# Residual stack of four layers: W1 on ScalarE's queue, the coefficient chain on GpSimd, transposes of the quantized quarters one product later

## The chip, the cores and the metric

The kernel runs on one core of a Trainium2 chip. The metric is the device time of one execution in microseconds (us); lower is better. Engines are named as in the profile: PE is TensorE, DVE is VectorE, ACT is ScalarE, POOL is GpSimd, SP is SyncE, which only issues transfers. Each runs its own list of instructions in order and waits on semaphores for the others.

## The reference, cut to what matters

`x` is (64, 64, 1024) in fp32: batch, head or row, position. Four layers each add to it:

```python
x = x + L0(x)   # y = irfft(rfft(u*mask) * rfft(K)), K = 2*einsum('hn,hnl->hl', Cs, exp(dtA*l)).real ; + u*D, masked
x = x + L1(x)   # x @ W1.T + 2 * (top-2 gated experts, each of rank 16: h = x @ A_e.T, then B_e)
x = x + L2(x)   # x @ W2.T + 0.5 * (x @ lora_A[label]) @ lora_B_w.T
x = x + L3(x)   # x @ w_eff.T
# L0: dt = exp(log_dt); A = -exp(log_A_real) + 1j*A_imag; dtA = A*dt; Cs = C*(exp(dtA)-1)/A     (64 x 64 each)
# L3: lora = B3 @ A3 ; wg = W3 + lora ; q = codebook[searchsorted(thresholds, wg/scale)]*scale ; w_eff = q + lora
```

## The kernel before

The three dense layers are linear in x, so the kernel multiplies their matrices once and then makes one pass over x. Up to about 370 us it builds the matrix and the tables of the convolution; after that it runs 32 alike tiles of two rows each.

**Preparation, in PE's order** (the list `order`, from which every engine takes its own part):

- `b3t` transposes B3; with A3 it gives the low-rank product of layer 3 in four quarters, `delta` (q = 0 to 3). It leaves in `dq`.
- `w2t` transposes a row block of W2 into `A2`; `qt(kt)` multiplies one column block of (1 + W2) by `E1` = (1 + W1 | 2·B_lang), 24 products: 16 of 512 columns, 8 of 128. The unit matrix is added by POOL, one 128x128 diagonal block at a time (`e1_ready`, `a2_ready`).
- `codesT`, `codes` sort out the code book; `nat4` transposes the four 64-column tables of layer 0; `at`, `wrt` transpose the expert matrices.
- `a3(q, n)` transposes the finished quarter q of the quantized matrix in four pieces, and `m(q, mt)`, ten products for each quarter, multiplies it into the final matrix `Mh`, `Ml`.
- Pieces leave PSUM through two alternating banks (`stage`): a piece waits until ACT has taken the one two before it.

**DVE** first works on the code book (`places_ready`), splits B3 and A3 (`b3_lo`), exponentiates the scale, then has a chain of about 70 instructions of 64x64 for layer 0 (lines 1376 to 1424, `exps`, `nat`, `nat4`), then the masks. Then come the four quarters of W3: two additions and a product over `vq`; for each code book step kept (here nine) two `TENSOR_SCALAR` (L1459) and two `TENSOR_TENSOR` (L1464) of 128x1024, here called the rises; a tail of four instructions (L1504, L1505). After the last quarter DVE builds the tables of layer 0 (`theta`, `rem`, `expo`) from `tabs`, together with sines and exponentials on ACT.

**POOL** adds the diagonals, and for quarters 0 to 2 runs `finish_quarter(q)`, three instructions that scale the quarter and add `dq`; `m_lo` is its subtraction behind each `m`. **ACT** takes pieces out of PSUM; `init_quarter(q)` fills the quarter's tile with the first code, and DVE's rises wait for it:

```python
                        if kt in (3, 4, 6):
                            init_quarter((3, 4, 6).index(kt) + 1)
```

**SP** issues all loads in the order of its code; W1's eight blocks come behind ten smaller loads.

Of the kernel before, what the change touches and what calls it, by code (L numbers as in the profile page):

```python
# [39 lines left out]
def resid_stack_kernel(nc, x, lengths, languages, labels, codebook, log_dt, C_ri, log_A_real, A_imag, D_skip,  # L40
# [96 lines left out]
    B3n = place("B3n", [P, NC, 2, R3], F32, at=region_q + 4 * (5 * QCOLS + 2 * 1024))  # L137
# [23 lines left out]
    nat = place("nat", [H, 16, N], F32, at=region_carry + 4 * 2 * EW)  # L161
    logs = place("logs", [H, 1 + N], F32)
# [3 lines left out]
    ex = place("ex", [P, 6, H + 1], F32)  # L166
    ex_bits = place("ex_bits", [P, H + 1], I32)
# [55 lines left out]
    with ExitStack() as ctx:  # L223
# [6 lines left out]
        ld_b3, ld_rank, ld_w1, ld_blang, ld_la = sem("ld_b3"), sem("ld_rank"), sem("ld_w1"), sem("ld_blang"), sem("ld_la")  # L230
# [6 lines left out]
        nat_rem, nat_sin, nat4_ready = sem("nat_rem"), sem("nat_sin"), sem("nat4_ready")  # L237
# [20 lines left out]
        order = [("b3t", 0), ("b3t", 1), ("codesT",)] + deltas(0) + [("w2t", 0, 0), ("w2t", 0, 1)]  # L258
        between = {0: [("codes",)], 1: [("nat4",), ("at", 0), ("at", 1), ("wrt",)], 2: deltas(1), 5: deltas(2), NC - 1: deltas(3)}
# [4 lines left out]
        order += [("a3", 0, n) for n in range(4)] + [("lap", mt) for mt in range(MT)]  # L264
# [5 lines left out]
        jobs = [j for j in order if j[0] not in ("qt", "m")]  # L270
# [61 lines left out]
        with nc.Block() as block:  # L332

            @block.sync
            def _(sp):
# [35 lines left out]

                load_w2(0)
                load_w2(1)
                for it in range(NC):
                    sp.dma_start(E1[:, it, L:EW].rearrange("p (e r) -> p e r", e=E),
                                 B_lang[:, it * P:(it + 1) * P, :].rearrange("e o r -> o e r")).then_inc(ld_blang, 16)
                for t in range(QT_TILES):
                    load_w3(0, t)
                sp.dma_start(len_i[:, :], bass.AP(lengths.tensor, 0, [[0, P], [1, B]])).then_inc(ld_ids, 16)
                for hh in range(HB):  # L380
                    rows = slice(hh * B, (hh + 1) * B)
                    sp.dma_start(ids_i[rows, 0:1], languages.rearrange("(b a) -> b a", a=1)).then_inc(ld_ids, 16)
                    sp.dma_start(ids_i[rows, 1:2], labels.rearrange("(b a) -> b a", a=1)).then_inc(ld_ids, 16)
# [55 lines left out]
            def _(pool):  # L439
# [74 lines left out]
                for it in range(NC):  # L514
# [11 lines left out]
                    if it == NC - 3:  # L526
                        finish_quarter(0)
# [60 lines left out]
            def _(pe):  # L588
# [1034 lines left out]
```

## Time and profile before

| | |
|---|---|
| median of 3 runs | 1046.71 us (1045.72 to 1048.4) |
| the profiled execution | 1049.61 us, of it 1047.8 us from first to last instruction (the span) |
| mean granted clock of TensorE | 0.992 |
| busy: PE, DVE, ACT, POOL | 1004.1, 850.6, 428.5, 292.0 us |

The span starts with the first instruction. All moments below are microseconds from there. A busy share is an average over the stages; what counts for a change is which engine another one waits for in its own stage.

### The profile page before, as it was taken

How to read it: one execution, taken by the hardware profiler on the slowest of the kernel's cores; microseconds unless marked ns; L12 is line 12 of the kernel's file. 1: busy time of each engine (PE TensorE's matmuls, PEld its weight loads, DVE VectorE, ACT ScalarE, POOL GpSimd, SP SyncE). 2: the span in 40 equal slices, each digit the busy share in tenths (PEclk: the TensorE clock that was granted, in tenths of full speed). 3: DMA queues.
4: the chain of work that ended last, by engine and by line, in shares of the span. 5: the costliest groups of instructions: out<-in, count | busy, mean ns of one | idle time of the engine just before them, and what ended most of it. 6: DMA issues, size and time to landing. Idle time of an engine off the chain costs nothing.

```text
span 1047.8 us, 16630 instructions
## 1 busy us (share of the span) xinstructions
PE 1004.1 (96%) x4855; PEld 800.8 (76%) x4855; DVE 850.6 (81%) x1678; ACT 428.5 (41%) x847; POOL 292.0 (28%) x319
## 2 busy tenths in 40 slices
PE   2999999999899999999999999999999999999997
PEld 1555556978688878888888888888888888888885
DVE  5888888979896488878888888888888888888862
ACT  3212222222257454454445444544354535553531
POOL 2200304373435323222332233222322232223100
PEclk9999999999999999999999999999999999999999
DMA  8601000010201335454544455445544454445311
GB/s 257 164 21 61 20 6 35 1 41 1 40 1 21 64 59 104 80 89 75 104 84 84 77 103 87 79 81 97 94 76 84 88 100 74 88 81 103 59 39 41
DMA packets 316659, 74.97 MB, mean 72 GB/s; under 512 B 292490, under 2 KB 309194, under 8 KB 316626
## 3 DMA queue, kind: packets, MB, share of 16 engines
q1 hardware_dynamic: 316626, 74.56, 36.2%
q8 instruction: 16, 0.26, 0.1%
q14 instruction: 17, 0.14, 0.0%
HBM read 57.61 MB, written 16.91 MB: 71 GB/s over the span
## 4 chain that ended last, share of the span: by engine, by line
PE 75%; DVE 10%; issue 9%; ACT 2%; DMA 2%; DVEq 1%; SPq 0%; ACTq 0%
PE bank L647 33%; PE bank L637 10%; PE bank L774 6%; PE bank L823 5%; PE bank L668 4%; PE bank L617 4%; PE bank L606 4%; PE bank L628 3%; DVE quant L1464 3%; PE bank L674 2%; DVE step_t L1459 1%; DVE quant L1505 1%; DVE vq L1478 1%; PE bank L658 1%; DVE quant L1504 1%
## 5 line engine op out<-in xcount | busy, mean ns | idle before, releaser
L647 PE MATMUL bank<-Mh,strips_r 128*128 128x512 f32 x1024 | 289.9, 395 | 0.0
L647 PEld LDWEIGHTS bank<-Mh,strips_r 128*128 128x128 f32 x1024 | 190.7, 188 | 41.5
L475 POOL TENSOR_TENSOR Cl<-QC,Ch 128x256 fp32r<-128x256 f32 x32 | 36.9, 1152 | 454.5 <-ACT Ch L879 454.5
L647 PE MATMUL bank<-Ml,strips_r 128*128 128x512 f32 x512 | 160.6, 395 | 0.0
L897 ACT ACTIVATE SK<-ZZ 64x448 f32<-64x448 f32 x128 | 73.9, 577 | 211.1 <-DVE ZZ L1182 208.7
L1182 DVE SCALAR_TENSOR_TENSOR ZZ<-ZZ,coef 128x192 f32<-128x192 f32 (+1 forms) x256 | 120.3, 510 | 10.1 <-DVE ZZ L1173 0.3
L774 PE MATMUL bank<-E,A 128*128 128x512 f32 (+1 forms) x384 | 126.2, 489 | 0.0
L647 PEld LDWEIGHTS bank<-Ml,strips_r 128*128 128x128 f32 x512 | 96.2, 188 | 22.5
L774 PEld LDWEIGHTS bank<-E,A 128*128 128x128 f32 x384 | 63.9, 192 | 61.8 <-issue 61.8
L637 PE MATMUL bank<-Mh,strips_r 128*128 128x296 f32 x512 | 110.5, 299 | 0.2 <-DVE strips_r L1201 0.2
L1464 DVE TENSOR_TENSOR quant<-quant,step_t 128x1024 f32<-128x1024 f32 x72 | 92.4, 1323 | 0.0
L637 PEld LDWEIGHTS bank<-Mh,strips_r 128*128 128x128 f32 x512 | 85.1, 189 | 5.4 <-issue 5.2
L1173 DVE SCALAR_TENSOR_TENSOR ZZ<-ZZ,coef 128x384 f32<-128x384 f32 (+1 forms) x128 | 80.3, 627 | 7.0 <-issue 1.0
L1459 DVE TENSOR_SCALAR step_t<-vq,steps 128x1024 f32<-128x1024 f32 x72 | 66.9, 970 | 21.7 <-DVEq L1499 13.1
L637 PE MATMUL bank<-Ml,strips_r 128*128 128x296 f32 x256 | 76.9, 300 | 0.0
L888 ACT ACTIVATE ZZ<-bank 64x448 f32<-64x448 f32 x128 | 68.5, 535 | 2.6 <-PE bank L606 0.3
L823 PE MATMUL bank<-A3b,QT 128*128 128x256 f32 x288 | 65.4, 387 | 3.7 <-ACT A3b L966 3.2
L823 PE MATMUL bank<-A3a,QT 128*128 128x256 f32 x288 | 65.2, 386 | 0.0
L823 PEld LDWEIGHTS bank<-A3b,QT 128*128 128x128 f32 x288 | 55.3, 194 | 12.0 <-ACT A3b L966 3.6
L1153 DVE TENSOR_TENSOR strips_r<-strips,strips_r 128x512 fp32r<-128x512 f32 x64 | 59.0, 924 | 5.7 <-ACT strips_r L867 5.7
L823 PEld LDWEIGHTS bank<-A3a,QT 128*128 128x128 f32 x288 | 55.5, 195 | 7.6
L1239 DVE TENSOR_TENSOR hgTl<-bank,hgTh 128x128 fp32r<-128x128 f32 x32 | 9.3, 292 | 61.3 <-ACT hgTh L918 61.3
(279 smaller groups left out, 1733.8 us busy)
## 6 DMA issues: line engine op xcount, KB each, us to landing
X<-in_x SPq DMA_DIRECT2D x256, 64.0 KB, 2.6
XT<-in_x SPq DMA_DIRECT2D x256, 64.0 KB, 2.5
out_x<-O SPq DMA_DIRECT2D x64, 256.0 KB, 3.2
toep<-kpad SPq DMA_DIRECT2D x128, 64.0 KB, 2.1
E<-in_L_cond_W SPq DMA_DIRECT2D x8, 512.0 KB, 7.4
W2s<-in_L_cond_W SPq DMA_DIRECT2D x8, 512.0 KB, 4.4
vq<-in_L_cond_weight SPq DMA_DIRECT2D x8, 512.0 KB, 3.3
LA<-in_L_cond_lora_A SPq DMA_DIRECT2D x8, 80.0 KB, 3.4
```

The costliest lines, as they stand in the source:

```text
L606: last = pe.matmul(psZ[hh][:, 0:SB].rearrange("p (c b) -> p c b", b=B), (Bh, Bl)[w][:, hh, :], (xh, xl)[p][:, 0:NC - 1, hh * B:(hh + 1) * ...
L637: last = pe.matmul(psL[:, 0:LOWC], xs[:, c, :], ms[:, c, L:MW], start=(c == 0 and n == 0), stop=False, skip_group_check=True)
L647: pe.matmul(psO[nh][:, :], xs[:, c, :], ms[:, c, nh * BANK:(nh + 1) * BANK], start=(c == 0 and n == 0), stop=False)
L774: last = pe.matmul(bank[s + n][:, 0:b - a], A2[:, it, kt * P:(kt + 1) * P], E1[:, it, a:b], start=(it == 0), stop=(it == NC - 1))
L823: last = pe.matmul(m_bank(n)[0:rows, 0:QO], lhs, A3[q % 2][:, kt, :], start=(kt == 0), stop=(kt == NC - 1))
L888: act.activation(ZZ[hh * N:(hh + 1) * N, :, ri, :], psZ[hh][ri * N:(ri + 1) * N, 0:SB].rearrange("p (c b) -> p c b", b=B), ACT.Copy).then_ ...
L897: act.activation(SK[ri * N:(ri + 1) * N, hh, :].rearrange("p (c b) -> p c b", b=B), ZZ[hh * N:(hh + 1) * N, :, ri, :], ACT.Copy).then_inc( ...
L1153: dve.tensor_tensor(xl[:, :, cols], xq[:, :, cols], xh[:, :, cols].bitcast(F32), ALU.subtract).then_inc(xl_done, 1)
L1173: dve.scalar_tensor_tensor(ZZ[:, dst, :, :], ZZ[:, src, :, :], coef[:, bass.ds(i, 1), power, 0], ZZ[:, dst, :, :], ALU.mult, ALU.add).then ...
L1182: dve.scalar_tensor_tensor(ZZ[:, dst, to, :], ZZ[:, src, of, :], coef[:, bass.ds(i, 1), power, n], ZZ[:, dst, to, :], ALU.mult, ALU.add).t ...
L1459: dve.tensor_scalar(step_t[:, c, :], vf[:, c * CH:(c + 1) * CH], kept_tau[:, bass.ds(k, 1)], rise[:, bass.ds(k, 1)], ALU.is_gt, ALU.mult). ...
L1464: dve.tensor_tensor(qf[:, cols], qf[:, cols], step_t[:, c, :], ALU.add).then_inc(dve_step, 1)
```

## The change

1. ACT issues W1's eight loads as its first instructions, each with its own semaphore `ld_w1[it]`. B3 is loaded once instead of twice, with 2 KB runs, and its copy of the transposed rows is made on ACT. SP's other loads change their order: W2 and W3 come ahead of `B_lang`, and the four loads of layer 0 come behind `B_lang`, after waits on `b3_lo` and `a3_pad`.
2. `qt(0)` is cut: `qt0(0)` multiplies blocks 0 to 3 of W1 as they come, ahead of `codesT` and `delta`; `qt0(1)` multiplies blocks 4 to 7 behind them.
3. Layer 0's chain leaves DVE for POOL as 90 instructions in four pieces (`nat_angles` 33, `nat_step` 30, `nat_products` 9, `nat_columns` 18; POOL's are split where DVE's did a product and an addition in one). Each piece stands between two of POOL's `a2_diagonal`. One reciprocal stays on DVE, ahead of quarter 1, behind a wait on `nat_den`. ACT's three sines move from behind `w2t(1)` to behind its take of `qt(1)`; `nat4` moves behind `qt(4)`.
4. `a3(q + 1, n)` stands behind `m` 3, 5, 7, 8 instead of 2, 4, 6, 8. `deltas(3)` moves behind `lap`. `init_quarter` moves from kt 3, 4, 6 to 3, 5, 7; `finish_quarter(0)` goes behind `a2_diagonal(5)`, `finish_quarter(2)` from behind `m(0, 4)` to behind `m(0, 8)`; `sines(0)` and `exponentials()` one product later.

```diff
-        order = [("b3t", 0), ("b3t", 1), ("codesT",)] + deltas(0) + [("w2t", 0, 0), ("w2t", 0, 1)]
-        between = {0: [("codes",)], 1: [("nat4",), ("at", 0), ("at", 1), ("wrt",)], 2: deltas(1), 5: deltas(2), NC - 1: deltas(3)}
+        order = [("b3t", 0), ("b3t", 1), ("w2t", 0, 0), ("w2t", 0, 1), ("qt0", 0), ("codesT",)] + deltas(0) + [("qt0", 1), ("codes",)]
+        between = {1: [("at", 0), ("at", 1), ("wrt",)], 2: deltas(1), 4: [("nat4",)], 5: deltas(2)}
...
-                if q + 1 < QUARTERS and mt in (2, 4, 6, 8):
-                    order += [("a3", q + 1, mt // 2 - 1)]
+                if q + 1 < QUARTERS and mt in (3, 5, 7, 8):
+                    order += [("a3", q + 1, (3, 5, 7, 8).index(mt))]
...
+                def exp_to(dst, src, w):
...
+                    step(pool.tensor_scalar(t[5], t[4], 1.0 / math.factorial(7), None, ALU.mult))
+                    for n in range(6, 0, -1):
+                        step(pool.tensor_scalar(t[5], t[5], 1.0 / math.factorial(n), None, ALU.add))
+                        step(pool.tensor_tensor(t[5], t[5], t[4], ALU.mult))
...
+                e1_diagonal(0)
+                e1_diagonal(1)
+
+                pool.wait_ge(e1_ready, 2)
+                pool.wait_ge(ld_a3, 32)
+                pool.tensor_tensor(A3lo[R3:, :], A3raw[R3:, :], A3raw[R3:, :], ALU.subtract).then_inc(a3_pad, 1)
+                pool.wait_ge(a3_pad, 1)
+                a2_diagonal(0)
+                for it in range(2, NC):
+                    e1_diagonal(it)
...
+                a2_diagonal(1)
+                pool.wait_ge(e1_ready, NC + 1)
+                pool.wait_ge(a2_ready, 2)
+                nat_angles()
+                a2_diagonal(2)
...
+                nat_step()
+                a2_diagonal(3)
+                pool.wait_ge(a2_ready, 4)
+                nat_products()
+                pool.wait_ge(nat_den, 1)
+                a2_diagonal(4)
+                pool.wait_ge(a2_ready, 5)
+                nat_columns()
+                a2_diagonal(5)
+                finish_quarter(0)
...
-                        if j == ("m", 0, 4):
+                        if j == ("m", 0, 8):
                             finish_quarter(2)
+                            pool.wait_ge(quant_done, 3)
...
+                for it in range(NC):
+                    act.dma_start(E1[:, it, 0:L], W1[it * P:(it + 1) * P, :]).then_inc(ld_w1[it], 16)
...
-                        if kt in (3, 4, 6):
-                            init_quarter((3, 4, 6).index(kt) + 1)
+                        if kt == 1:
+                            nat_sine()
+                        elif kt in (3, 5, 7):
+                            init_quarter(kt // 2)
...
+                    if q == 1:
+                        dve.wait_ge(nat_den, 1)
+                        dve.reciprocal(nat[:, 7, :], nat[:, 15, :]).then_inc(nat_inv, 1)
```

**PE at its start, before.** `ident` is the unit matrix used for transposes, `E_84` is `E1`, `A_85` is `A2`; ahead of these rows stand `b3t`, `codesT` and the first two `delta` pieces.

```order
L728 MATMUL bank<-A3hh,B3s 128x512 [waits stage_free]
L728 MATMUL bank<-A3lo,B3s 128x512
L733 MATMUL bank<-ident,W2s 128x128 [waits stage_free,ld_w2a]
L733 MATMUL bank<-ident,W2s 128x128 x3
L733 MATMUL bank<-ident,W2s 128x128 [waits stage_free]
L733 MATMUL bank<-ident,W2s 128x128 x3
L733 MATMUL bank<-ident,W2s 128x128 [waits stage_free,ld_w2b]
L733 MATMUL bank<-ident,W2s 128x128 x3
L733 MATMUL bank<-ident,W2s 128x128 [waits stage_free]
L733 MATMUL bank<-ident,W2s 128x128 x3
L774 MATMUL bank<-E_84,A_85 128x512 [waits stage_free,a2_ready,e1_ready]
L774 MATMUL bank<-E_84,A_85 128x512 x15
```

The same place with the change:

```order
L852 MATMUL bank<-ident,W2s 128x128 [waits stage_free]
L852 MATMUL bank<-ident,W2s 128x128 x3
L887 MATMUL bank<-E_84,A_85 128x512 [waits e1_ready,stage_free,a2_ready]
L887 MATMUL bank<-E_84,A_85 128x512
L887 MATMUL bank<-E_84,A_85 128x512 [waits e1_ready]
L887 MATMUL bank<-E_84,A_85 128x512
L887 MATMUL bank<-E_84,A_85 128x512 [waits e1_ready]
L887 MATMUL bank<-E_84,A_85 128x512
L887 MATMUL bank<-E_84,A_85 128x512 [waits e1_ready]
L887 MATMUL bank<-E_84,A_85 128x512
L858 MATMUL bank<-ident,cbw 64x128 [waits stage_free,places_ready]
L858 MATMUL bank<-ident,tau 64x128
```

Half of the first block's 512-column products now stands ahead of `codesT`; the eight `delta` products follow, then the other half, then `codes`.

**POOL at the diagonals of A2, before**: nothing stands between the diagonals of blocks 2 to 5 (the row with x4) and the finish of quarter 0.

```order
L517 TENSOR_TENSOR A_85<-A_85,ident 128x128 [waits stage_free]
L525 TENSOR_SCALAR Bw_64<-BwIn 128x8x32 [waits ld_rank]
L525 TENSOR_SCALAR Bw_64<-BwIn 128x8x32 x2
L517 TENSOR_TENSOR A_85<-A_85,ident 128x128 [waits stage_free] x4
L502 TENSOR_TENSOR quant_70<-quant_70,scale_82 128x1024 [waits v_used]
```

With the change, the end of `nat_step`, the diagonal of block 3, and the start of `nat_products`:

```order
L561 TENSOR_TENSOR nat<-nat 64x64 [waits pool_step]
L562 TENSOR_SCALAR nat<-nat 64x64 [waits pool_step]
L563 TENSOR_TENSOR nat<-nat 64x64 [waits pool_step]
L564 TENSOR_SCALAR nat<-nat 64x64 [waits pool_step]
L565 TENSOR_TENSOR nat<-nat 64x64 [waits pool_step]
L611 TENSOR_TENSOR A_85<-A_85,ident 128x128 [waits stage_free,pool_step]
L568 TENSOR_TENSOR nat<-c_in,nat 64x64 [waits a2_ready]
L569 TENSOR_TENSOR nat<-c_in,nat 64x64 [waits pool_step]
```

Block 3's diagonal, for which `qt(3)` waits, now stands behind 67 other instructions since the diagonal of block 1: 33 of `nat_angles`, block 2's diagonal, three of `Bw`, 30 of `nat_step`.

## Rows read from the trace of the kernel before

**Rows 1.** Page, part 1: busy time of each engine, share of the span, instructions.

```profile
PE 1004.1 (96%) x4855; PEld 800.8 (76%) x4855; DVE 850.6 (81%) x1678; ACT 428.5 (41%) x847; POOL 292.0 (28%) x319
```

**Rows 2.** Chain of work, 286 to 290 us: start, us, what.

```profile
286.26 2.71 DVE quant L1511
289.01 1.12 PE bank L790 x4
```

**Rows 3.** Timeline of PE: start, us, instruction, count, idle before and releaser.

```profile
21.16 0.79 PE L728 MATMUL bank<-A3hh,B3s 128*128 128x512 f32 x1 [1.65 <-DVE A3lo L1368]
28.19 15.68 PE L774 MATMUL bank<-E,A 128*128 128x512 f32 x48
45.88 15.68 PE L774 MATMUL bank<-E,A 128*128 128x512 f32 x48
...
66.33 13.90 PE L774 MATMUL bank<-E,A 128*128 128x512 f32 x30
...
87.21 15.68 PE L774 MATMUL bank<-E,A 128*128 128x512 f32 x48
...
236.47 10.63 PE L823 MATMUL bank<-A3b,QT 128*128 128x256 f32 x48 [3.15 <-ACT A3b L966]
...
289.01 1.12 PE L790 MATMUL bank<-ident,quant 128*128 128x128 f32 x4 [5.63 <-DVE quant L1511]
289.92 8.77 PE L823 MATMUL bank<-A3a,QT 128*128 128x256 f32 x32
...
298.96 7.07 PE L823 MATMUL bank<-A3a,QT 128*128 128x256 f32 x32
```

**Rows 4.** Timeline of DVE up to the rises of quarter 1, same columns.

```profile
26.62 0.19 DVE L1309 TENSOR_SCALAR ex<-logs 64x65 f32<-64x65 f32 x1
45.08 0.18 DVE L1429 CAST len_f<-len_i 128x64 f32<-128x64 int32 x1
48.48 2.49 DVE L1478 TENSOR_TENSOR vq<-vq,dq 128x1024 f32<-128x1024 f32 x2 [1.03 <-issue]
55.18 1.53 DVE L1459 TENSOR_SCALAR step_t<-vq,steps 128x1024 f32<-128x1024 f32 x2 [1.89 <-DVEq L1499]
97.04 1.22 DVE L1505 TENSOR_TENSOR quant<-quant,vq 128x1024 f32<-128x1024 f32 x1
107.58 2.30 DVE L1459 TENSOR_SCALAR step_t<-vq,steps 128x1024 f32<-128x1024 f32 x1 [2.18 <-DVEq L1499]
```

**Rows 5.** Busy time by stretch: the nine rises of quarters 0 to 3.

```profile
55.18:93.39 38.21, 36.09 (x134) 20.23 (x133) 34.02 (x37) 8.44 (x18) 1.62 (x2) 0.96 0.04 15
107.58:153.18 45.60, 44.41 (x143) 22.76 (x142) 41.67 (x36) 8.43 (x15) 10.55 (x5) 1.00 0.00 1
235.35:278.38 43.03, 41.91 (x202) 36.53 (x203) 39.10 (x37) 10.88 (x31) 18.12 (x17) 1.00 0.14 22
```

**Rows 6.** Timeline of POOL: one instruction alone, and the same kinds beside DVE.

```profile
21.27 3.40 POOL L513 TENSOR_TENSOR E<-E,ident 128x128 f32<-128x128 f32 x8 [10.68 <-DMA E<-in_L_cond_W]
66.40 1.17 POOL L517 TENSOR_TENSOR A<-A,ident 128x128 f32<-128x128 f32 x1 [20.04 <-ACT A L966]
175.82 1.92 POOL L543 TENSOR_TENSOR A3a<-A3a,ident 128x128 f32<-128x128 f32 x2 [8.71 <-ACT A3a L966]
332.02 0.61 POOL L452 TENSOR_TENSOR QB<-X1T,rem 128x256 f32<-128x256 f32 x1 [2.07 <-ACT coef L991]
```

**Rows 7.** Timeline of DVE beside POOL at 175 and at 220 us.

```profile
175.75 1.67 DVE L1459 TENSOR_SCALAR step_t<-vq,steps 128x1024 f32<-128x1024 f32 x2
220.02 2.80 DVE L1505 TENSOR_TENSOR quant<-quant,vq 128x1024 f32<-128x1024 f32 x1
226.13 5.24 DVE L1478 TENSOR_TENSOR vq<-vq,dq 128x1024 f32<-128x1024 f32 x1 [2.18 <-DMA vq<-in_L_cond_weight]
```

**Rows 8.** Timeline of ACT: the fill of quarter 1.

```profile
104.06 1.92 ACT L1009 ACTIVATE quant<-cb 128x2048 f32<-128x2048 f32 x1
```

**Rows 9.** Timeline of DVE: the second half of the tables.

```profile
320.11 1.56 DVE L1533 SCALAR_TENSOR_TENSOR rem<-theta 128x1344 f32<-128x1344 f32 x1 [3.13 <-ACT turns L975]
```

More of the change, by code:

```diff
@@ L159, in resid_stack_kernel @@
     Vt = place("Vt", [P, H, SPAN], F32, at=region_q - 4 * NC * QO)
[L161 to L162 removed]
+    logs = place("logs", [H, 1 + N], F32, at=region_q + 4 * (6 * QCOLS + 2 * 1024))
     exps = place("exps", [H, 1 + N], F32)
@@ L263, in resid_stack_kernel @@
             order += [("qt", kt)] + between.get(kt, [])
-        order += [("a3", 0, n) for n in range(4)] + [("lap", mt) for mt in range(MT)]
+        order += [("a3", 0, n) for n in range(4)] + [("lap", mt) for mt in range(MT)] + deltas(3)
         for q in range(QUARTERS):
@@ L758, in wrt, with qt0 @@
                     several(("wrt",), NC, lambda ps, c: pe.transpose(ps[:, c * E:(c + 1) * E], Wr_nat[:, c * P:(c + 1) * P], ident[0:E, 0:E]))
+                def qt0(part):
+                    if part == 0:
+                        pe.wait_ge(a2_ready, 1)
+                        pe.wait_ge(stage_free, jobno[("w2t", 0, 1)] + 1)
+                    for it in range(part * NC // 2, (part + 1) * NC // 2):
+                        pe.wait_ge(e1_ready, it + 1)
+                        for n in range(2):
+                            pe.matmul(bank[2 + n][:, :], A2[:, it, 0:P], E1[:, it, n * BANK:(n + 1) * BANK], start=(it == 0), stop=(it == NC - 1))
                 def qt(kt):
-                    if kt == 0:
-                        pe.wait_ge(e1_ready, NC)
                     pe.wait_ge(a2_ready, kt + 1)
@@ L824, in m @@
                     last.then_inc(m_full, 1)
-                do = dict(b3t=b3t, delta=delta, w2t=w2t, codesT=codes_t, codes=codes, nat4=nat4_t, at=at, wrt=wrt, qt=qt, lap=lap,
+                do = dict(b3t=b3t, delta=delta, w2t=w2t, codesT=codes_t, codes=codes, nat4=nat4_t, at=at, wrt=wrt, qt0=qt0, qt=qt, lap=lap,
                           a3=a3, m=m)
@@ L998, in _ @@
                 lo_n, hi_n = slice(0, N), slice(N, 2 * N)
+                for it in range(NC):
+                    act.dma_start(E1[:, it, 0:L], W1[it * P:(it + 1) * P, :]).then_inc(ld_w1[it], 16)
                 def nat_sine():
@@ L1013, in _ @@
                     if name == "b3t":
-                        take(j, B3raw[:, which[0] * BANK:(which[0] + 1) * BANK], stage(j)[0:2 * R3, :], scale=0.5)
+                        blocks = slice(4 * which[0], 4 * which[0] + 4)
+                        act.wait_ge(stage_full, jobno[j] + 1)
+                        for rows in (slice(0, R3), slice(R3, 2 * R3)):
+                            last = act.activation(B3raw[rows, :].rearrange("r (p t) -> r t p", t=NC)[:, blocks, :],
+                                                  stage(j)[0:R3, :].rearrange("r (t p) -> r t p", t=4), ACT.Copy, scale=0.5)
+                        last.then_inc(stage_free, 1)
                         if which[0] == 1:
@@ L1425, in _ @@
-                last.then_inc(nat4_ready, 1)
                 dve.wait_ge(ld_ids, 80)
```

218 lines of the change are left out of this document (126 added, 92 removed).

## The prediction

> **What bounds the kernel now.** I read the page first: PE is busy 96% of the span, DVE 81% [rows 1]. So the 32 tiles behind 370 us, which the change does not touch, are PE's, and only the 370 us of preparation can move. For these I read the chain of waits and then the timelines of PE, DVE, POOL and ACT side by side. The chain shows that preparation ends on DVE: its last addition for quarter 3 starts at 286.26, and PE's transposes of that quarter start at 289.01 [rows 2], after 5.63 us without work [rows 3]. PE has another stop of 3.15 us at 236.47 [rows 3]: ACT holds the last piece of `a3` back while POOL finishes quarter 2. Behind the 5.63 us the next two products take 8.77 us instead of 7.07, and the transposes 1.12 [rows 3]: 2.2 us more that the stop costs. Up to 289 PE and DVE are thus two strings of nearly the same length, PE's about 11 us shorter. A gain must come to both.
>
> DVE's string hangs on PE's in one place. The rises of quarter 1 start at 107.58 [rows 4], and the fill of their tile, which ACT does behind `qt(3)`, runs from 104.06 for 1.92 us [rows 8]: 1.6 us from its end to the rises.
>
> **Part 1: the opening.** Before, PE starts its first `delta` at 21.16, when DVE has split A3, and `qt(0)` at 28.19 [rows 3]. After, 16 of its 24 products are split in two, and the first half, about 7 us of the 15.68, stands in the idle time ahead of the `delta` pieces. The loads of W1 now run beside the scale's, for which DVE starts; I allow 1 us for that. PE: `delta` 22.2 to 26, second half to 33, `codes`, `w2t(1)`, the rest of `qt(0)` and `w2t(2)` to about 40; `qt(1)` starts there instead of at 45.88 [rows 3], about 6 us earlier. That `codes` is now free of `qt(0)`'s end, and that the chain of 26.62 to 45.08 has left DVE (18.5 us) [rows 4], brings DVE to quarter 0 at about 35.8 instead of 48.48: 12.7 us earlier.
>
> One rule speaks against moving W1: the Trainium skill, "DMA: Bandwidth & Descriptors", section "Rules for kernel authors", says that spreading transfers over several queues gives no bandwidth, only issue time. By it W1 cannot come early without making the scale late; if that took 3 us instead of 1, the sum below would be 2 us higher.
>
> **Part 2: the chain on POOL.** It starts with the diagonal of block 1, at about 35.5, so it lies beside DVE's quarter 0. What does one of its 64-column instructions take there? No row shows one. Alone, eight of 128 columns take 3.40 us, 0.43 each, and one of 256 takes 0.61 [rows 6]; for 64 I take 0.38 with its semaphore. Beside rises it is otherwise: the 128-column addition that met a DVE addition at 66.40 took 1.17, and two in a row at 175.82 took 1.92 [rows 6], while the DVE pair beside them took 1.67 instead of 1.53 [rows 7, 4]. Each time POOL's ends some 0.3 us after DVE's instruction does. So beside rises I count one POOL instruction for one of DVE's, and DVE loses little, 0.05 to 0.1 us each.
>
> Quarter 0 lasts from 48.48 to 98.26 [rows 4], 49.8 us, with 43 long DVE instructions (3, 36, 4), and about 7 us of gaps (1.89 ahead of the rises and 1.03 before the quarter [rows 4], 38.21 less 34.02 within the rises [rows 5]), in which 13 fit. So POOL does about 56 in 52.5 us. From this:
>
> - `nat_rem`, its 33rd: 30 us, at 66. ACT, in order, stands at its sines since `qt(1)` ended at 55.5; PE stops at `wrt`, two stage banks on. The sines, the take of `at`, then `wrt` and `w2t(3)` are some 4 of the 4.8 us that lie between the two blocks before (45.88 + 15.68 to 66.33 [rows 3]); with 2 us for a slow restart, as at 289, `qt(2)` starts at about 72, not 66.33. With 20.9 us from there to `qt(3)` (87.21 less 66.33) [rows 3] PE would be ready at 93.
> - Block 3's diagonal is the 68th: 12 are left when DVE's quarter ends at 88.3. DVE then waits for `nat_den`, and POOL goes at 0.4: 35.8 + 58.5 = 94.3.
> - So `qt(3)` starts at about 94.5, against 87.21: **+7.3**. DVE has `nat_den` at 98, and could start rises at 106, but ACT's fill comes behind `qt(3)`: rises at 107.58 + 7.3 = 114.9. DVE's 12.7 us are gone, and 7.3 more.
>
> The bounds of this step: with no wait at all, block 3's diagonal is early and `qt(3)` starts at 81 (-6); with a POOL instruction 15% dearer and a late opening, at 101 (+14). I take the middle, since both rows beside rises agree with one for one.
>
> **Part 3: behind `qt(3)`.** `nat_columns` lies in DVE's wait and costs nothing. `finish_quarter(0)` again meets the first rises (45.60 against 38.21 us for nine [rows 5]): 7.4 us, as before. `finish_quarter(2)` leaves the seam of quarters 2 and 3, where it made 1.22 into 2.80 and 5.24 [rows 4, 7], 5.6 us, and lands in the rises of quarter 3, 7.4 us: +1.8. Of the 4.8 us that subtractions cost those rises (43.03 against 38.21 [rows 5]) I take off 0.8. DVE is done at 289.0 + 7.3 + 1.0 = 297.3. PE, without the 3.15, arrives at the transposes at about 291.5 with one product more behind it: it waits again, but has 3.45 us less to do afterwards. **+7.3 + 1.0 - 3.45 = +4.85.** The tables follow DVE's end, +8.3, less the 3.13 us in which DVE waited for the sines [rows 9]: +5.2, as much as PE's. I cost the rest at nothing: `deltas(3)` is the same work for PE at either place and DVE wants it only at quarter 3's start, some 25 us later; the sines and exponentials one product later stand where PE, too, is one product further. If quarter 3 came as early as the first rival has it, that cover would still be over 10 us.
>
> The profiled execution has a span of 1047.8 and a time of 1049.61, the runs a median of 1046.71. +4.8 gives a span of 1052.6, and against the median **1051.5**.
>
> **The rivals.**
>
> - **The chain hides (faster).** If POOL gets two instructions in beside one of DVE's, `nat_rem` is there at 51, no engine stops, and `qt(3)` starts at 81: -6 + 1.0 - 3.45 = -8.4, 1038.3. For it: POOL's instructions are short. Against it: both of a pair at 175.82 waited. It decides below 0.6 us each. Chance 0.18.
> - **The instructions are cheaper, the queueing holds.** At 0.30 us each the gaps take more of them: `qt(3)` at 89.5, shift +2.3, end -0.2: no change, 1046.5. [...] No row here shows 64 columns. Chance 0.28.
> - **The opening slips as well (slower still).** If W1 beside SP's loads holds the scale, W2's block 2 or layer 0's loads back by 5 us, all of part 2 starts later: +10, 1056.7. Chance 0.12.
> - My forecast: 0.42.
>
> 0.3% is 3.1 us, about what a measurement tells from no change. Faster: the first rival and a little, 0.2. Same: the second and the forecast's lower edge (its own range 1047.5 to 1056), 0.3. Slower: 0.5. The range takes in the first rival's value and the last's: 1037.5 to 1059.
>
> **What would show it.** In the profile after: `qt(1)` from about 40 and quarter 0 from about 36 (part 1); POOL's 64-column rows at about 1 us beside rises and 0.4 when DVE stands; PE idle before `wrt` by about 10 us, behind ACT's sines; DVE idle before its reciprocal by about 10 us, with POOL as releaser; rises of quarter 1 at about 115; PE idle before the first transpose of quarter 3 by 5 us. I am wrong if POOL's rows are at 0.4 to 0.6 beside rises: then PE doesn't stop at `wrt`, and the end is earlier by up to 13 us.

## The result, and the profile after

The changed kernel takes 1070.96 us (median of 4 runs, 1067.71 to 1075.32) where the kernel before takes 1046.86 beside it: a ratio of 1.0232, interval 1.0191 to 1.0273. It is slower by 24 us. The forecast was 1051.5, with 1059 as the end of its range. The profiled execution has a span of 1070.4 and a time of 1072.25.

The page's busy line of the changed kernel, which answers to [rows 1]:

```profile
PE 1010.1 (94%) x4855; PEld 805.8 (75%) x4855; DVE 835.7 (78%) x1613; ACT 431.4 (40%) x849; POOL 351.5 (33%) x409
```

PE's share fell from 96 to 94% in a longer span. Of the 22.6 us by which the span grew, 16.6 are idle time of PE, and 6.0 are the same 4855 products taking longer (1010.1 against 1004.1 us busy, at a mean granted clock of 0.978 against 0.992). So the place to look is where PE stops, and how it starts again. PE's timeline of the changed kernel (start, time taken, engine, line, operation, count, and in brackets the idle time before it with what ended it), as [rows 3]:

```profile
17.27 10.16 PE L887 MATMUL bank<-E,A 128*128 128x512 f32 x16 [4.77 <-POOL A L611]
29.46 0.30 PE L858 MATMUL bank<-ident,cbw 128*64 128x128 f32 x1 [2.04 <-DVE cbw L1501]
32.69 0.79 PE L847 MATMUL bank<-A3hh,B3s 128*128 128x512 f32 x1 [2.71 <-DVE A3lo L1507]
36.47 7.32 PE L887 MATMUL bank<-E,A 128*128 128x512 f32 x16
47.89 15.68 PE L903 MATMUL bank<-E,A 128*128 128x512 f32 x48
83.69 1.02 PE L877 MATMUL bank<-ident,Wr_nat 8*128 8x8 f32 x8 [19.24 <-ACT AT L1095]
86.40 16.60 PE L903 MATMUL bank<-E,A 128*128 128x512 f32 x48
107.33 15.68 PE L903 MATMUL bank<-E,A 128*128 128x512 f32 x48
...
160.83 0.50 PE L847 MATMUL bank<-A3hh,B3s 128*128 128x512 f32 x1 [2.69 <-ACT dq L1095]
198.07 1.97 PE L919 MATMUL bank<-ident,quant 128*128 128x128 f32 x8 [2.75 <-ACT A3a L1095]
225.29 0.80 PE L847 MATMUL bank<-A3hh,B3s 128*128 128x512 f32 x1 [2.28 <-ACT dq L1095]
```

Three things are to be seen. The first `delta` stands at 32.69, 11.5 us later than before, with half of `qt(0)` now in front of it. PE stops for 19.24 us ahead of `wrt`. And three stops of 2.3 to 2.8 us that were 0.91 or less now stand before `deltas(2)`, `a3(0)` and `deltas(3)`. `qt(3)` starts at 107.33 against 87.21 [rows 3]: 20.1 of the 22.6 us of span are lost by then.

The first of these stops has a fill of ACT in front of it (ACT's timeline of the changed kernel: the fill of quarter 2, then the take for which PE waits):

```profile
158.37 1.92 ACT L1140 ACTIVATE quant<-cb 128x2048 f32<-128x2048 f32 x1
160.17 1.10 ACT L1095 ACTIVATE dq<-bank 128x512 f32<-128x512 f32 x2
```

Why the opening is late: DVE's timeline of the changed kernel, as [rows 4], and then its table of transfers (size in KB, median us from issue to landing):

```profile
21.07 0.41 DVE L1471 SCALAR_TENSOR_TENSOR cbw<-cb 128x64 f32<-128x64 f32 x1 [21.07 <-DMA scale<-in_L_cond_scale_log]
46.39 2.48 DVE L1571 TENSOR_TENSOR vq<-vq,dq 128x1024 f32<-128x1024 f32 x2 [1.03 <-ACT A L1095]
109.14 0.55 DVE L1567 RECIPROCAL nat<-nat 64x64 f32<-64x64 f32 x1 [11.54 <-POOL nat L576]
```

```profile
E<-in_L_cond_W ACTq DMA_DIRECT2D x8, 512.0 KB, 13.4
A3raw<-in_L_cond_lora_A SPq DMA_DIRECT2D x2, 256.0 KB, 11.2
B3n<-in_L_cond_lora_B SPq DMA_DIRECT2D x1, 256.0 KB, 4.6
scale<-in_L_cond_scale_log SPq DMA_DIRECT2D x1, 32.0 KB, 17.5
```

`scale3` is issued at 3.6 us and lands at 21: 17.5 us for 32 KB, beside W1's 4 MB on the other queue (before, 5.2 us). DVE's whole string begins there.

Why PE stops at `wrt`: POOL's timeline of the changed kernel. The chain starts behind block 1's diagonal; the angles are done at 82.2:

```profile
45.67 0.46 POOL L611 TENSOR_TENSOR A<-A,ident 128x128 f32<-128x128 f32 x1 [12.38 <-ACT A L1095]
49.20 2.25 POOL L514 TENSOR_SCALAR nx<-nx 64x65 f32<-64x65 f32 x1
66.18 3.00 POOL L529 TENSOR_TENSOR nx<-nx 64x65 f32<-64x65 f32 x1
82.28 0.79 POOL L611 TENSOR_TENSOR A<-A,ident 128x128 f32<-128x128 f32 x1
98.71 0.36 POOL L528 TENSOR_SCALAR nx<-nx 64x64 f32<-64x64 f32 x1
99.15 0.31 POOL L529 TENSOR_TENSOR nx<-nx 64x64 f32<-64x64 f32 x1
105.17 0.46 POOL L611 TENSOR_TENSOR A<-A,ident 128x128 f32<-128x128 f32 x1
```

The 33 instructions of the angles take 35.9 us beside DVE's quarter 0: one starts every 1.09 us, and a single one takes up to 3.00. Once DVE stands (it waits from 97.6 to 109), the two shown take 0.31 and 0.36, and one starts every 0.4 us.

PE's clock in the stretches of the opening (us, PE's busy time and count, granted clock, share of DMA, GB/s):

```profile
50.00:75.00 25.00, 14.45 (x52) 0.86 0.03 10
75.00:100.00 25.00, 16.31 (x46) 0.74 0.17 60
```

Both stretches hold a mixture of the two levels, 2.4 and 1.2 GHz: within the stop, from 70 to 83.7, and under `wrt` and `w2t(3)`, up to 86.4, the granted clock was 0.50, and from 90 on it was 1.00. `qt(2)` starts at the low level and takes 16.60 us where an undisturbed block takes 15.68. But that is no loss against the kernel before, where it took 16.55.

### The profile page after: what moved, and what is told of

Its sections match the earlier page's. It is cut to its first block, busy times and chain, and to the rows that moved or that the text cites. A ratio compares the mean times of both kernels' runs of the same rounds, so it can differ in the third digit from the quotient of the medians.

```text
span 1070.4 us, 16667 instructions
## 1 busy us (share of the span) xinstructions
PE 1010.1 (94%) x4855; PEld 805.8 (75%) x4855; DVE 835.7 (78%) x1613; ACT 431.4 (40%) x849; POOL 351.5 (33%) x409
## 4 chain that ended last, share of the span: by engine, by line
PE 87%; POOL 3%; ACT 2%; DVE 1%; issue 1%; DMA 0%; SPq 0%; DVEq 0%; ACTq 0%; POOLq 0%
PE bank L766 32%; PE bank L952 13%; PE bank L756 10%; PE bank L903 9%; PE bank L787 4%; PE bank L736 4%; PE bank L725 3%; PE bank L747 3%; PE bank L911 2%; PE bank L793 2%; PE bank L777 1%; POOL nx L528 1%; POOL nx L529 1%; PE bank L919 1%; PE bank L714 1%
## 5 line engine op out<-in xcount | busy, mean ns | idle before, releaser
L482 POOL TENSOR_TENSOR Cl<-QC,Ch 128x256 fp32r<-128x256 f32 x32 | 34.6, 1081 | 457.1 <-ACT Ch L1008 457.1
L766 PEld LDWEIGHTS bank<-Ml,strips_r 128*128 128x128 f32 x512 | 96.2, 188 | 22.6
L903 PE MATMUL bank<-E,A 128*128 128x512 f32 (+1 forms) x352 | 112.5, 480 | 0.0
L1554 DVE TENSOR_TENSOR quant<-quant,step_t 128x1024 f32<-128x1024 f32 x72 | 100.6, 1437 | 0.0
L903 PEld LDWEIGHTS bank<-E,A 128*128 128x128 f32 x352 | 57.9, 192 | 54.1 <-issue 54.1
L952 PEld LDWEIGHTS bank<-A3b,QT 128*128 128x128 f32 x288 | 55.9, 196 | 10.6 <-issue 2.9
L674 POOL TENSOR_TENSOR Ml<-m,Mh 128x256 fp32r<-128x256 f32 x32 | 42.2, 1320 | 59.1 <-ACT m L1224 58.9
```

What stands on the lines that cost most here:

```text
L766: pe.matmul(psO[nh][:, :], xs[:, c, :], ms[:, c, nh * BANK:(nh + 1) * BANK], start=(c == 0 and n == 0), stop=False)
L903: last = pe.matmul(bank[s + n][:, 0:b - a], A2[:, it, kt * P:(kt + 1) * P], E1[:, it, a:b], start=(it == 0), stop=(it == NC - 1))
L952: last = pe.matmul(m_bank(n)[0:rows, 0:QO], lhs, A3[q % 2][:, kt, :], start=(kt == 0), stop=(kt == NC - 1))
L1554: dve.tensor_tensor(qf[:, cols], qf[:, cols], step_t[:, c, :], ALU.add).then_inc(dve_step, 1)
```

## The experiments

The kernels of one comparison ran beside the kernel before, which took 1046.5 to 1047.1 us in all of them.

**1. Scale first (1070.88; ratio 1.0227, 1.0202 to 1.0252).** The changed kernel with

```diff
+                sp.dma_start(scale3[:, :, :], scale_log.rearrange("(t p) g a -> p t (g a)", p=P)).then_inc(ld_codes, 16)
+                sp.dma_start(cb[:, :], bass.AP(codebook.tensor, 0, [[0, P], [1, K_CODES]])).then_inc(ld_codes, 16)
                 sp.dma_start(B3n[:, :, :], B3_lora.rearrange("(p t) r -> p t r", t=NC)).then_inc(ld_b3, 16)
```

and the two lines taken out where they stood, in front of W2's block 0 and of the weights.

> The changed kernel with one thing moved: the loads of scale3 and of the codebook are the first two that SP issues, ahead of B3n and W2. Theory O (the opening: scale3 lands 12 us late beside the 4 MB of W1, and every one of those us is paid, since the whole chain of quantization and tables starts behind it): VectorE's first instruction is at about 9 us instead of 21.1, quarter 0's first load is used at 36 instead of 46.4, the third quarter's product qt(3) comes at about 97 instead of 107.3, and the time is 1060 us (1057 to 1063). Theory C (the chain on GpSimd costs by itself, and the late start is hidden in it): VectorE starts at 9 us as well, but the time stays at 1068 to 1071. Theory M (the moves behind the first 100 us cost the time): 1068 to 1071 too.

Its table of transfers, and one row each of its POOL and PE timelines:

```profile
scale<-in_L_cond_scale_log SPq DMA_DIRECT2D x1, 32.0 KB, 4.2
B3n<-in_L_cond_lora_B SPq DMA_DIRECT2D x1, 256.0 KB, 8.4
A3raw<-in_L_cond_lora_A SPq DMA_DIRECT2D x2, 256.0 KB, 12.9
...
42.43 0.46 POOL L611 TENSOR_TENSOR A<-A,ident 128x128 f32<-128x128 f32 x1 [9.11 <-ACT A L1095]
...
84.03 1.02 PE L877 MATMUL bank<-ident,Wr_nat 8*128 8x8 f32 x8 [22.82 <-ACT AT L1095]
```

DVE starts at 7.8, 13 us earlier, and nothing comes of it. B3n and A3raw are now what lands late: PE starts `b3t` at 10.4 instead of 5.4, and the first half of `qt(0)` at 21.4 instead of 17.3. Quarter 0 and the chain start 3.3 us earlier (43.1 and 43.0), but the angles take 39.5 us instead of 35.9, and `qt(3)` starts at 108.6, later than in the changed kernel. Theory O as I had put it (the scale alone) falls.

**2. W1 on SP (1066.67; 1.0192, 1.0172 to 1.0211).** The eight loads of W1 stand on SP behind `scale3`'s instead of on ACT.

> The changed kernel with W1's eight loads issued by SP again, directly behind scale3's, instead of by ScalarE at once; all else as in the changed kernel. Theory O: scale3 lands at about 10 us since nothing large is ahead of it but 512 KB of W2, the time is 1058 to 1064. Theory C or M: it stays at 1067 to 1072. If W1's early start is worth something by itself, this one comes out slower than the kernel with scale3 first by that much: I expect 0 to 3 us, since TensorE waited on the codes and not on W1 there.

Block 1's diagonal on POOL, then `wrt` on PE:

```profile
38.36 0.46 POOL L613 TENSOR_TENSOR A<-A,ident 128x128 f32<-128x128 f32 x1 [4.81 <-ACT A L1097]
...
77.03 1.02 PE L879 MATMUL bank<-ident,Wr_nat 8*128 8x8 f32 x8 [14.84 <-ACT AT L1097]
```

The chain starts 7.3 us earlier, `qt(3)` 5.5 us earlier (101.79), and the time falls by 4.3 us: W1's place is paid for, but this is a fifth of the loss, and a smaller gain than Theory O had (1058 to 1064). W1's early issue buys no earlier start: here `qt(0)`'s first half starts at 16.54, earlier than in the changed kernel.

**3. The moves alone (1049.92; 1.0027, 1.0014 to 1.0040).** The kernel before with

```diff
-        between = {0: [("codes",)], 1: [("nat4",), ("at", 0), ("at", 1), ("wrt",)], 2: deltas(1), 5: deltas(2), NC - 1: deltas(3)}
+        between = {0: [("codes",)], 1: [("nat4",), ("at", 0), ("at", 1), ("wrt",)], 2: deltas(1), 5: deltas(2)}
...
-        order += [("a3", 0, n) for n in range(4)] + [("lap", mt) for mt in range(MT)]
+        order += [("a3", 0, n) for n in range(4)] + [("lap", mt) for mt in range(MT)] + deltas(3)
...
-                if q + 1 < QUARTERS and mt in (2, 4, 6, 8):
+                if q + 1 < QUARTERS and mt in (3, 5, 7, 8):
-                        if j == ("m", 0, 4):
+                        if j == ("m", 0, 8):
                             finish_quarter(2)
-                        if kt in (3, 4, 6):
+                        if kt in (3, 5, 7):
```

and the sines and exponentials one product later. `finish_quarter(2)` waits for `quant_done` as in the changed kernel.

> The kernel before with the third part of the change alone: quarters transposed one product later (behind products 3, 5, 7 and 8), deltas(3) behind the low-rank products, finish_quarter(2) behind m(0,8), the quarters' fills behind qt(3), qt(5) and qt(7), the sines one product later. Theories O and C: nothing beyond 3 us either way, 1044 to 1050: the stall of 3.45 us before the first transposes goes, and finish_quarter(2) costs some of it beside the rises of quarter 3. Theory M: slower by 8 to 20 us, 1055 to 1067.

PE's timeline:

```profile
136.34 0.79 PE L729 MATMUL bank<-A3hh,B3s 128*128 128x512 f32 x1 [2.70 <-ACT dq L967]
174.73 1.14 PE L791 MATMUL bank<-ident,quant 128*128 128x128 f32 x8 [2.75 <-ACT A3a L967]
199.37 0.50 PE L729 MATMUL bank<-A3hh,B3s 128*128 128x512 f32 x1 [2.28 <-ACT dq L967]
```

Slower by 3 us, at the edge of "no change". The stops of 3.15 and 5.63 us at 236 and 289 [rows 3] are gone as predicted; in their place stand the same three stops as in the changed kernel. The fills of quarters 2 and 3, 1.9 us each, are now in ACT's queue right ahead of the takes of `deltas(2)` and `a3(0)`, and `deltas(3)` comes behind ACT's copies of the low-rank tables. The profiled execution is the fastest of the ten (1045.62 us), so its rows show the stops, but not what makes the median 3 us slower.

**4. The chain back on DVE (1065.98; 1.0176, 1.0146 to 1.0206).** The changed kernel with the chain's code of before on DVE, its inputs loaded behind `scale3`'s, and the tables where they lay before.

> The changed kernel with the tables' chain back on VectorE, its four inputs loaded behind scale3's and kept where they were before, the turned tables taken behind qt(1) as before; W1 from ScalarE's queue and the moves stay. Loading scale3 first had started VectorE 13 us earlier and gained nothing, so the opening alone is not what is paid. Theory C (the chain on GpSimd holds ScalarE's sines and A2's blocks, and with them TensorE at the last rank transpose until 84): without it TensorE has no stop of 19 us there, qt(3) comes at about 88, and the time is 1046 to 1054, though VectorE's quarter 0 starts only at 55 to 60. Rival D (with the late scale3, the chain on VectorE pushes the rises so far that VectorE's last quarter sets the end of the first part): 1055 to 1062. Rival O+M (neither engine of the chain matters): 1068 or more.

DVE's quarter 0 and PE's first transpose of quarter 3:

```profile
63.61 2.49 DVE L1515 TENSOR_TENSOR vq<-vq,dq 128x1024 f32<-128x1024 f32 x2 [1.03 <-issue]
...
303.34 1.12 PE L817 MATMUL bank<-ident,quant 128*128 128x128 f32 x4 [4.62 <-DVE quant L1548]
```

Theory C is right on the stop (PE has none at `wrt`) and wrong on the price: quarter 0 now starts at 63.6, and DVE's last quarter sets the transposes of quarter 3 14 us later than before (303.34 against 289.01). Rival D had the mechanism and gave too little.

**5. W1 on SP as well (1057.80; 1.0108, 1.0084 to 1.0131).** The same with W1 on SP behind the small loads, and W2's block 1 ahead of the weights.

> The chain on VectorE, with W1 on SP behind the small loads, and the second block of W2 ahead of the weights: against the run with the chain on VectorE and W1 from ScalarE's queue (1066) this is the price of the late scale3 where VectorE has the chain. Theory O: scale3's 10 us are paid one for one, as VectorE is in a chain of 27 us and 4 quarters behind it: 1052 to 1057. If they are not paid, 1063 or more, and the price lies in the products split around the codes (TensorE at half clock there) or in the moves.

8.2 us come back, and quarter 0 starts at 56.9. The scale lands some 10 us earlier, so with the chain on DVE most of the late opening is paid.

**6 to 8. What waits behind the chain.** Three edits of the changed kernel, which leave the chain on POOL: ACT's sines behind `qt(2)` instead of `qt(1)`; POOL's diagonals of blocks 2 and 3 and Bw3 ahead of pieces of the chain; and both together, with the sines behind `qt(3)`. The last one's core, POOL's waits left out:

```diff
                 a2_diagonal(1)
+                a2_diagonal(2)
-                nat_angles()
+                nat_exps()
-                a2_diagonal(2)
...
+                a2_diagonal(3)
+                nat_turns()
+                nat_dens()
+                a2_diagonal(4)
+                nat_mag()
                 nat_step()
-                a2_diagonal(3)
                 nat_products()
-                a2_diagonal(4)
+                a2_diagonal(5)
                 nat_columns()
-                a2_diagonal(5)
+                a2_diagonal(6)
                 finish_quarter(0)
-                a2_diagonal(6)
...
-                        if kt == 1:
+                        if kt == 3:
                             nat_sine()
```

`nat_exps` and `nat_turns` are the two halves of `nat_angles`; `nat_mag` and `nat_dens` are what was the beginning of `nat_step` and the end of `nat_products`.

> The changed kernel with ScalarE's nat_sine moved from behind the copy of qt(1) to behind that of qt(2), so that ScalarE takes the turned A_nat and Wr blocks without waiting for the angles. A2's block 2 still gets its diagonal behind the angles, at 82 us. Theory C: TensorE's stop only moves from the last rank transpose (83.7) to qt(2), which starts at 82.3 to 83 instead of 86.4; but block 3's diagonal now waits for sines that come behind qt(2)'s copy, so qt(3) starts at 105 to 108, and the time is within 4 us of the changed kernel's 1071. A theory by which ScalarE's wait alone is the stop: qt(2) at 66 and a time of 1055.

> The changed kernel with GpSimd's queue in another order: A2's block 2 gets its diagonal ahead of the chain, Bw3 is written behind the first exponential, block 3's diagonal follows the angles, and den (which needs only the exponential) is computed ahead of the second exponential, its reciprocal written over it; nat_sine stays behind the copy of qt(1). Theory C: ScalarE still waits for the angles, which come 3 to 6 us later than in the changed kernel (Bw3 and one diagonal are now ahead of them), so TensorE's stop lasts to 86 to 90; behind it qt(3) no longer waits for the second exponential. qt(3) at 107 to 112, the time 1068 to 1075. A theory by which the diagonals alone are the stop: 1055.

> Both at once: GpSimd's order as in the kernel with the diagonals first, with the diagonals of blocks 3 and 4 moved up further, ahead of the angles and of the second exponential; nat_sine behind the copy of qt(3), the turned tables taken behind qt(5), and quarter 2's fill behind qt(6) (it is written over the tables). The chain stays on GpSimd, instruction for instruction, and is as slow beside the rises. Theory C: nothing waits for the chain any more, TensorE runs through from qt(1) to qt(4), qt(2) starts at about 69 and qt(3) at about 90 instead of 107.3, and the time is 1050 to 1056 (1071 less 17, give or take 3). If it stays above 1062, the chain is not what holds the kernel, and what GpSimd takes from the rises or the late scale3 is.

Measured: 1075.86 (1.0277, 1.0239 to 1.0315), 1088.05 (1.0380, 1.0355 to 1.0405) and 1061.62 (1.0130, 1.0103 to 1.0157). PE's stops, sines late:

```profile
82.55 18.16 PE L903 MATMUL bank<-E,A 128*128 128x512 f32 x48 [16.32 <-POOL A L611]
```

diagonals first:

```profile
92.43 1.02 PE L889 MATMUL bank<-ident,Wr_nat 8*128 8x8 f32 x8 [27.78 <-ACT AT L1107]
```

and both:

```profile
87.38 15.68 PE L915 MATMUL bank<-E,A 128*128 128x512 f32 x48
...
127.03 18.57 PE L915 MATMUL bank<-E,A 128*128 128x512 f32 x48 [6.71 <-POOL A L618]
...
153.53 0.79 PE L859 MATMUL bank<-A3hh,B3s 128*128 128x512 f32 x1 [5.58 <-ACT dq L1107]
```

PE is held by the chain in two ways, and to free one alone gains nothing: with the sines late it waits for block 2's diagonal, with the diagonals first for the sines. Diagonals first was 13 us above the end of what I expected: the chain starts behind block 2's diagonal, at 51.7 instead of 46.3, Bw3 takes 4.8 us within it, so the angles end at 90.9 instead of 82.2, and the turned tables then cost PE another stop of 5.05 us. With both, `qt(3)` starts at 87.38, where it stood before the change, though the chain is as slow as it was. But 1061.62 lies above the 1050 to 1056 expected, and just under the 1062 beyond which I would have given the theory up. The rows show two stops of its own making: block 5's diagonal stands behind `nat_step` and `nat_products`, which POOL works at without a pause, and `finish_quarter(0)` stands behind the whole chain.

**9 to 11. Its own stops taken out.** In turn: `a2_diagonal(5)` and `finish_quarter(0)` ahead of `nat_step`, the turned tables behind `qt(6)`, the fills of quarters 2 and 3 both behind `qt(7)`; then W1 on SP, and W2's block 1 ahead of the weights; then the moves undone as well.

> The kernel with both edits (GpSimd's diagonals ahead of the chain's pieces, the sines behind qt(3)) with the two stops taken out that its own order had made: A2's block 5 gets its diagonal and quarter 0 is finished ahead of the wait for the sines, block 6's ahead of the last piece, the turned tables are taken behind qt(6), and quarters 2 and 3 are filled behind qt(7). The chain stays on GpSimd whole, and scale3 still lands late (21 us). Theory C (all that the chain on GpSimd costs is what waits behind it): the stops of 6.7 us before qt(5) and 5.6 us in deltas(2) go, and the time is 1048 to 1052, where 1061.6 was measured with them. Theory P (the chain takes time from the rises through the port, so that VectorE becomes the bound): 1056 or more, with a wait for quant of over 6 us before the last quarter's transposes.

> The same with W1's eight loads on SP directly behind scale3's, and the second block of W2 ahead of the weights' quarter 0. Theory O (once nothing waits for the chain, the late scale3 is paid): VectorE's first instruction at 11 instead of 21 us, quarter 0 at 38 to 40 instead of 46.5, qt(1) at 41 to 42 instead of 47.5, and the time falls by 5 to 7 us, to 1042 to 1046. If the opening is hidden even now, it is the same within 2 us.

> The same with the third part of the change undone: quarters transposed behind products 2, 4, 6 and 8, deltas(3) behind qt(7), finish_quarter(2) behind m(0,4), the sines a product earlier. By the run of the moves alone they are worth between 1 and 4 us against, so this is 1 to 4 us faster than the kernel with them; where VectorE's quarter 2 comes late (finish_quarter(2) behind m(0,4) then holds GpSimd), it is equal or slower by up to 3.

Measured: 1056.14 (1.0091, 1.0058 to 1.0123), 1052.99 (1.0065, 1.0044 to 1.0085), 1052.31 (1.0044, 1.0031 to 1.0058). Each gives back less than I expected. By its time alone the first falls to Theory P (1056 or more), but PE's wait for `quant` is 4.84 us, not over 6; the runs of the fills below decide it. The second one's DVE timeline shows what still stood in the way, at the rises of quarter 1:

```profile
107.14 3.14 DVE L1564 TENSOR_SCALAR step_t<-vq,steps 128x1024 f32<-128x1024 f32 x2 [10.41 <-DVEq L1607]
```

DVE is ready for them at 96.7 and waits 10.4 us for the quarter's fill, which ACT does behind `qt(3)` and, in my order, behind the sines. In the first two the double fill behind `qt(7)` also makes the stop before `a3(0)` 4.55 us, 2.75 in the changed kernel.

**12 to 14. The fills moved.** The last kernel with

```diff
-                        if kt == 3:
-                            nat_sine()
-                        if kt == 3:
+                        if kt == 2:
                             init_quarter(1)
-                        if kt == 7:
-                            init_quarter(2)
+                        elif kt == 3:
+                            nat_sine()
+                        elif kt == 7:
                             init_quarter(3)
```

quarter 2's fill behind the take of the turned tables, and W2's block 1 ahead of W1. Then the same with W1 on ACT and the changed kernel's order of loads; and the first with the moves back in.

> The freed kernel without the moves (1052.3), with quarter 1's fill behind the copy of qt(2) instead of behind qt(3) and the sines, quarter 2's behind the turned tables, quarter 3's behind qt(7), and the second block of W2 ahead of W1. If the fills are what is left: VectorE's wait of 10.4 us before the rises of quarter 1 falls to about 2, quarter 3 is done at about 280 instead of 289.5, TensorE's waits of 5.3 us for quant, 4.5 us in deltas(3) and about 3 of 3.7 us for W2 go, and the time is 1040 to 1044, below the kernel before. If the chain on GpSimd takes as much from the rises as it saves (port), VectorE's quarter 3 is still done at 287 or later and the time is 1048 or more.

> The same with W1's loads on ScalarE's queue at once, and SP's order of loads, as in the changed kernel: scale3 lands at 21 us again. If the late scale3 is paid one for one: 8 to 10 us more than with W1 on SP. If TensorE is the bound once VectorE is early enough, only what TensorE's own opening loses is paid, 2 to 4 us more: qt(1) at 47 to 48 instead of 40 to 42, less the wait that then stands before it.

> The kernel with the fills moved, with the third part of the change in it again (quarters transposed one product later, deltas(3) behind the low-rank products, finish_quarter(2) behind m(0,8), sines a product later). With VectorE early, no transpose waits for a quarter in either, so the later transposes gain nothing and the moves cost what they cost TensorE: the same within 3 us, likelier 1 to 3 us slower, from finish_quarter(2) beside quarter 3's rises and the last products' wait of 2.4 us.

Measured: **1044.07 (0.9966, 0.9952 to 0.9981)**, 1050.73 (1.0026, 1.0014 to 1.0037) and 1047.59 (1.0003, 0.9990 to 1.0017). The first is below both kernels, by 3 us against the one before, and Theory P falls with it. Quarter 0 on DVE and the first transpose of quarter 3 on PE in it:

```profile
39.31 2.48 DVE L1585 TENSOR_TENSOR vq<-vq,dq 128x1024 f32<-128x1024 f32 x2 [1.02 <-ACT A L1108]
...
99.11 1.53 DVE L1563 TENSOR_SCALAR step_t<-vq,steps 128x1024 f32<-128x1024 f32 x2 [1.20 <-DVEq L1606]
...
282.94 0.66 PE L932 MATMUL bank<-ident,quant 128*128 128x128 f32 x4 [0.24 <-DVE quant L1618]
```

and that transpose with W1 on ACT:

```profile
289.44 1.12 PE L930 MATMUL bank<-ident,quant 128*128 128x128 f32 x4 [4.36 <-DVE quant L1618]
```

So the chain on POOL need cost nothing, and DVE is early: the stop of 5.63 us of [rows 3] is 0.24. How much of the 3 us comes from the chain's new place isn't shown, since the kernel before was not run with its fills moved. W1 on ACT, with that order of loads, costs 6.7 us here, and the moves cost 3.5.

## Why the prediction was wrong

The sign was right and the size was a fifth. Three terms of the sum failed; everything is in spans of the profiled executions (predicted +4.8, measured +22.6).

- **"The loads of W1 now run beside the scale's, for which DVE starts; I allow 1 us for that."** This step failed first and cost most. The scale landed 12.1 us later (21.07 against 8.99), and `codesT` waits for DVE and stands ahead of `deltas(0)`, the rest of `qt(0)` and `w2t(1)` in PE's order. So the opening moved against the forecast: `qt(1)` at 47.89 instead of 40 (7.9 us), quarter 0 at 46.4 instead of 35.8 (10.6), the chain's start at 46.3 instead of 35.5 (10.8). It isn't the scale alone: loaded first, it was replaced by B3n and A3raw (experiment 1). Nor is it W1's queue alone. With W1 behind the small loads (experiment 2) the chain starts at 39.0, which gives back 7.3 of the 10.8. The other 3.5 stay, since `delta` now stands behind the first half of `qt(0)`: "about 7 us" were given to it, it took 10.16 (10.02 in experiment 2), and there `delta` starts behind it at 26.6, not at 22.2. The rival "the opening slips as well" was this mechanism, with 5 us where 11 came. The rule of the Trainium skill that I weighed against the move ("DMA: Bandwidth & Descriptors", "Rules for kernel authors") pointed the right way, and my 3 us beside it were too few.
- **"`nat_rem`, its 33rd: 30 us".** It took 35.9. In that time DVE did 31 long instructions, so one for one was right; but the 13 that I had fit into DVE's gaps were about 6, and POOL had done 49 and not 56 when DVE's quarter ended at 97.6. That block 3's diagonal came 58.9 us after the chain's start where I had 58.5 is partly luck: the forecast's own terms, 88.3 and twelve of 0.4, give 93.1 and not 94.3. `qt(2)` started at 86.4 where 72 was forecast, 10.8 of it the late start. PE then reached `qt(3)` after the diagonal (105.2), not before it, at 107.33 instead of 94.5: 12.8 us more, by the timeline 10.8 of the late start and 2 of this. By experiment, 5.5 of it are shown to belong to W1's place (experiment 2).
- **"it waits again, but has 3.45 us less to do afterwards"** (PE) and **"I cost the rest at nothing"** in part 3. The forecast had DVE set the end, at 297.3, with PE waiting 5 us before the first transpose of quarter 3. DVE ended at 309.0 and PE, held before, came later still, at 314.06, without a stop. So the end went by PE's own string. The stops of 3.15 and 5.63 us went, with their slow restart 11.0 us. But I looked for cover of `deltas(3)` and the sines only on DVE and PE, and didn't cost the fills behind `qt(5)` and `qt(7)` in ACT's queue, nor a slow restart behind new stops: three stops of together 7.7 us where 2.1 were (+5.6), the 144 products behind the second of them in 21.92 us instead of 19.80 (granted clock 0.90 against 1.00), a stop of 2.47 us at 339.17 where 0.54 stood at 317.81, and about 4 in smaller pieces. Behind `qt(3)` the span grew by 2.5 us, where I had -2.45. Measured by itself the part is +3 (experiment 3) and +3.5 (experiment 14).

4.8 + 12.8 + 5.0 is the 22.6 that was measured.

`finish_quarter(2)` was nearly as predicted: DVE's row beside it, with POOL's two rows, in the changed kernel:

```profile
262.10 4.64 POOL L509 TENSOR_TENSOR quant<-quant,scale 128x1024 f32<-128x1024 f32 x2
266.82 5.38 POOL L510 TENSOR_TENSOR quant<-quant,dq 128x2048 f32<-128x2048 f32 x1
...
264.91 8.38 DVE L1554 TENSOR_TENSOR quant<-quant,step_t 128x1024 f32<-128x1024 f32 x2
```

8.38 us for a pair that takes 2.35 undisturbed, and the rises of quarter 3 last 50.4 us instead of 43.0: the 7.4 of the forecast, without the 0.8 that it took off.

The mechanism of part 2 stands: PE stops at `wrt` behind ACT's sines, and DVE idles before its reciprocal (11.5 us; "about 10"). PE's stop is twice the "about 10 us": 19.24, since the angles took 5.9 us more and the chain's start slipped by 2.9 us more than `qt(1)`. The rival by which the chain hides had POOL get two instructions in beside one of DVE's, and no run shows that; its outcome, a chain that costs nothing, came in experiment 12 by another way, once nothing that PE needs stood behind the chain. The rival of cheaper instructions was right on their price and wrong on what it does. A 64-column instruction takes 0.23 to 0.37 us when DVE stands, around the 0.30 of that rival. Beside the rises one starts for about one of DVE's, and its own price doesn't matter.

What stays open: whether the small loads wait for the wires, for the queue's service or for their memory in front of W1. No run here tells these apart. Nor was the chain on POOL tried with the undivided `qt(0)` of before.

## What to carry to other kernels

When a long chain moves to an engine that was idle, don't ask first what it costs there, but list everything that stands behind it in that engine's queue and behind each of its readers in theirs. Here both a diagonal on POOL and a take on ACT held PE, and only freeing both gave time back. A bulk load that is moved to a free queue has a price in the small loads that others start with. A fill or a copy "costed at nothing" is a stop about as long as itself if it lands in a queue just ahead of a take that the bound engine waits for (fills of 1.92 us made stops of 0.91 and 0.25 into 2.69 and 2.75). And after each wait that is removed, look at the next one: in the freed kernel DVE stood 10.4 us for a fill that had been in nobody's way, and moving the fills (with one load of W2) gave 8.2 us.

## What the runs showed of the hardware

- Beside 4 MB in eight loads on ACT's queue, a load of 32 KB on SP's took 17.5 us from issue to landing (5.2 before, 7.5 with W1 behind it on SP, 4.2 when it was issued first). The two loads of 256 KB ahead of it took 11.2 (median; 5.4 before, 7.5 with W1 on SP), and 12.9 when the scale was issued ahead of them.
- A POOL instruction of 64 or 65 columns beside DVE's quarter 0 took 0.24 to 3.00 us, and one started every 1.09 us. DVE paid little for it: the rises of quarter 0 lasted 39.9 us with the chain beside them, 38.2 without. With POOL's long instructions (1024 and 2048 columns) it was DVE that paid, 7.4 us for 10.
- After an idle stretch products ran at half pace though their stretch shows the full granted clock. PE's timeline of the changed kernel at both ends of `qt(0)`'s first half, and the windows (us, PE's busy time and count, granted clock, share of DMA, GB/s):

```profile
17.27 2.08 PE L887 MATMUL bank<-E,A 128*128 128x512 f32 x2 [4.77 <-POOL A L611]
...
23.83 3.60 PE L887 MATMUL bank<-E,A 128*128 128x512 f32 x8
```

```profile
17.00:20.00 3.00, 2.73 (x4) 1.00 1.08 373
23.00:25.00 2.00, 2.00 (x5) 1.00 1.17 215
```

The products of the first row start 1.0 us apart and those of the second 0.43, both with 1.00 in the clock's column (the 2.4 GHz level); before them PE had stood for 4.77 us. The transfers beside them are not the reason, as far as experiment 12 shows: there the same products are 0.43 us apart from 21.5 us on, while over 400 GB/s are moved. So the 16 took 10.16 us and the other 16, later, 7.32: idle time filled with products gives back less than their usual duration.
